# Position tables over 194 distinct columns, and table pieces of five and three tiles, in a DeBERTa-style attention kernel

## The chip, the cores and the metric

The kernel runs on one core of a Trainium2 chip. The metric is the device time of one execution in microseconds (us). The kernel before was timed three times: 1996.8 us in the median, from 1993.77 to 2002.08 us.

## What is computed

A sandwich layer over x of shape (4, 1024, 256) in fp32: attention with relative positions inside two layer norms, then a mixture of eight experts chosen by argmax inside two more. What matters here is the attention's position term, for 16 heads of 16 channels:

```python
scores = einsum('bhqd,bhkd->bhqk', q, k) / scale
rel = log_bucket(q_index - k_index)            # exact up to 32, logarithmic up to 127, then flat
c2p = take_along_axis(q @ pos_k.T, clip(rel + 64, 0, 127))
p2c = take_along_axis(k @ pos_k.T, clip(-rel + 64, 0, 127)).swapaxes(-1, -2)
probs = softmax(scores + (c2p + p2c) / scale)
ctx = einsum('bhqk,bhkd->bhqd', probs, v)
```

`rel` depends on the distance alone. Between distances -31 and 31 the reference puts every distance into one and the same bucket, so the position term is flat there; beyond 127 it is a constant on each side.

## The kernel before

The program is five blocks that run one after the other: `spread` (position rows), `project` (q, k, v), `attend`, `mix` (output projection, norms, routing) and `experts`. The change lies in `spread` and `attend`.

**The unit of work in attend.** A unit n is one (batch, head) pair; there are 64, each of eight tiles of 128 queries (or keys). Scores have a band: for query tile t the key tiles t-1, t, t+1 need the position term by distance, and all others take the constant of their side through extra rows of the bf16 products. A step s of the main loop stands for tile t = s % 8 of unit n = s // 8.

**Tables.** For a tile of 128 queries (and one of 128 keys) PE multiplies with the picked position rows and gets, for 255 distances and one far column, two tables of 128 x 256 in PSUM (`make_table`, L703 to L715). This runs 16 steps ahead of the scores (AHEAD). ScalarE (ACT) copies both tables to SBUF (`keep_table`, L852 to L859), between the two halves of the exponent of another tile.

**The skew.** A table holds distances; a score tile needs them by key, shifted by one column a row. The shift is made through DRAM: SyncE (SP) writes tables to `skew_d` (`skew_write`) and reads them back with a row pitch one element shorter (`skew_read`) into `near`. A unit has two pieces: the writes cover tiles 0 to 3 and 4 to 7 (1024 KB each), the reads tiles 0 to 2 and 3 to 7 (384 KB and 640 KB for each of two tables). In what follows W0, W1 are the two writes of a unit and R0, R1 the two reads (each of two DMAs). SP's order in a round u (L677 to L695) is R1 of unit u+1, W0 of u+2, the loads of unit u+4, the store of u-2, R0 of u+2, W1 of u+2. SP handles one DMA after the other and stands at each wait: a read waits until its write has landed in DRAM (`skew_out`, L662), a write until its last tile's table is copied (`table_kept`, L651).

**Edges.** GpSimd (POOL) makes the triangular edges of `near` in five operations for each piece (`edge`, steps 0 to 4), the first behind the read's landing (`skew_in`, L925); the tuple `steps` (L964) says at which step s of the round each is put in POOL's order. At t = 7 POOL also splits the row maxima of the unit into three bf16 parts (`split_top`), behind whatever edge operations stand before it.

**Scores and probabilities.** PE makes the scores of step s (`score`), adds `near` for keys by transposing products (L740, which waits for the piece's edges by `near_made`), VectorE (DVE) finds the maxima and adds `near` for queries (`look`, `level`), and 13 steps later PE turns the result (`flip`), ACT takes the exponent in two halves of 512 (`exponent`), and PE multiplies with v (`weigh`, one step later). The maxima come back as three rows of the products: at t = 1 PE turns the split maxima of the unit before (`turn_top`, L782, which waits for `split_made` and shares `table_ps` with the tables) and ACT copies them (`keep_top`).

PE's order in a step is flip half 0, a table, flip half 1, scores, weigh, and at t = 1 `turn_top`. Each engine runs its own list in order and stands at each wait.

Of the kernel before, what the change touches and what calls it, by code (L numbers as in the profile page):

```python
# [30 lines left out]
BAND = 2 * P - 1  # L31
PARTS = 3
# [21 lines left out]
def constants():  # L54
# [14 lines left out]
    pick[:, right, BAND] -= 1  # L69
    k, m = np.arange(P)[:, None], np.arange(P)[None, :]  # L70
# [19 lines left out]
def build(nc, x, Wq, bq, Wk, bk, Wv, bv, Wo, bo, rel_emb, ln_s, ln_b, W1, b1, W2, b2, Wr, br,  # L90
          c_pick, c_masks, c_fold, c_side, c_steps, c_sel, out):
    ctx = ExitStack()
    with ctx:
# [10 lines left out]
        pick_d = dram("pick_d", [KROWS, H * 4 * P], BF16)  # L104
# [64 lines left out]
def spread(nc, sem, Wk, bk, rel_emb, c_pick, c_masks, c_side, pick_d, posT_d):  # L169

    with ExitStack() as ctx:
# [8 lines left out]
        pick = sb("pick", [P, 2, 2 * P])  # L180
# [17 lines left out]
        def _(sp):  # L198
# [9 lines left out]
            for tab in range(2):  # L208
                for n, (first, step, many) in enumerate((KSLOTS, QSLOTS)[tab]):
                    for slot in range(first, first + step * many, step):  # L210
                        for c in range(2):
                            sp.dma_start(view(pick_d, slot * (DH * H * 4 * P) + c * 8 * 4 * P + tab * 2 * P,
                                              [[4 * P, 8], [H * 4 * P, DH], [1, 2 * P]]),
                                         part[:, n, tab, c, :]).then_inc(stored, 16)
# [4 lines left out]
        def _(pe):  # L219
# [10 lines left out]
            for c in range(2):  # L230
                nc.tensor.transpose(posT_ps[:, c, :], pos[:, c * P:(c + 1) * P], ident)
                for tab in range(2):
                    last = nc.tensor.matmul(pick_ps[:, tab, c, :], pos[:, c * P:(c + 1) * P], pick[:, tab, :],
# [4 lines left out]
        def _(act):  # L238
# [7 lines left out]
            for tab in range(2):  # L246
                last = nc.scalar.copy(pick32[:, tab, :, :], pick_ps[:, tab, :, :])
# [307 lines left out]
def attend(nc, sem, spent, c_masks, split_d, far_d, v_d, pick_d, skew_d, ctx_d):  # L555
# [12 lines left out]
    PIECES = ((0, 3), (3, QT))  # L568
    EDGES = ((0, 3), (3, QT - 1))
# [4 lines left out]
    with ExitStack() as ctx:  # L574
# [10 lines left out]
        rows = sb("rows", [KROWS, H, 2, 2 * P], BF16)  # L585
        vals = [sb(f"vals{i}", [P, QT, VROW]) for i in range(2)]
        table = [sb(f"table{i}", [P, 2, 2, 4, SPOT]) for i in range(2)]
# [41 lines left out]
        def _(sp):  # L629
# [20 lines left out]
            def skew_write(n, h):  # L650
                sp.wait_ge(table_kept, n * QT + 4 * h + 4)  # L651
                if n >= 2:
                    sp.wait_ge(skew_in[n % 2][0], 16 * 2 * (n // 2))
                    sp.wait_ge(skew_in[n % 2][1], 16 * 2 * (n // 2))
                sp.dma_start(view(skew_d, n % 2 * (P * PITCH) + h * 4 * SPOT + 1, [[PITCH, P], [TABLE, 2], [1, 4 * SPOT]]),
                             table[n % 2][:, h, :, :, :].rearrange("p a u v -> p a (u v)")).then_inc(skew_out[n % 2][h], 16)

            def skew_read(n, h):
                if n >= 2:
                    sp.wait_ge(scored, (n - 2) * QT + 4 * h + 4)  # L660
                    sp.wait_ge(seen, (n - 2) * QT + 4 * h + 4)
# [38 lines left out]
        def _(pe):  # L700
            ident = masks[:, 4, :]

            def make_table(x):  # L703
# [8 lines left out]
                nc.tensor.matmul(table_ps[:, 0, :], quest[i][0:KROWS, u * P:(u + 1) * P], rows[:, n % H, 0, :],  # L712
                                 start=True, stop=False)
                nc.tensor.matmul(table_ps[:, 1, :], after[i][0:KROWS, u * P:(u + 1) * P], rows[:, n % H, 1, :],  # L714
# [925 lines left out]
```

## Time and profile before

| | us |
|---|---|
| median of three runs | 1996.8 |
| lowest, highest | 1993.77, 2002.08 |
| the profiled execution | 2003.63 |
| its span, first to last instruction | 2001.7 |
| PE busy | 1698.0 (85%) |
| DVE busy | 1370.7 (68%) |
| ACT busy | 1121.8 (56%) |
| POOL busy | 1069.1 (53%) |
| q1, SP's DMA queue, share of 16 DMA engines | 65.2% |

The profiled execution is one of its own, 1.9 us longer than its span. "Busy" of PE counts matmuls in flight, which overlap. The tables begin at 215 us and the last weighted sum of attend is copied at about 1490 us, so attend takes 1275 us of the 2002.

### The profile page before, as it was taken

The numbers are of one execution on the slowest core, as the hardware profiler recorded it, in microseconds if no ns is written. First come the engines' busy times: TensorE is split into PE (matmuls) and PEld (weight loads), VectorE is DVE, ScalarE is ACT, GpSimd is POOL, SyncE is SP. The second block draws the span as 40 slices with busy tenths as digits, with TensorE's granted clock in tenths as the row PEclk, the third lists the DMA queues.
The fourth block names the chain that finished last, engine by engine and source line by source line (L and its number), as shares of the span: only waits on it lengthen the run. The fifth ranks groups of instructions, "written<-read, shape, count | busy, mean of one in ns | idle before, by whom it ended". The sixth has DMA issues, their size and how long they took to land. (4 is left out here: it accounts for less than half of the span.)

```text
span 2001.7 us, 40568 instructions
## 1 busy us (share of the span) xinstructions
PE 1698.0 (85%) x13688; PEld 1159.6 (58%) x13688; DVE 1370.7 (68%) x3938; ACT 1121.8 (56%) x2233; POOL 1069.1 (53%) x1268
## 2 busy tenths in 40 slices
PE   1882389999999999999999999999973674999997
PEld 1451156565656566566565666566532464999996
DVE  1673188788888788898798899899843553343343
ACT  1672257676767677677677777677751460222221
POOL 0210267676777667667576777777711451233332
PEclk6996589999999999999999999999996675999998
DMA  4598778777777777777877777787718852676772
GB/s 113 188 303 274 225 250 262 246 237 251 245 261 248 256 247 240 257 254 245 265 237 251 249 261 250 240 272 246 235 44 215 284 176 86 198 212 215 223 219 78
DMA packets 320826, 453.36 MB, mean 226 GB/s; under 512 B 35132, under 2 KB 260303, under 8 KB 320526
## 3 DMA queue, kind: packets, MB, share of 16 engines
q1 hardware_dynamic: 308034, 415.25, 65.2%
q10 hardware_dynamic: 7596, 21.10, 3.4%
q0 software_dynamic: 4992, 14.43, 1.9%
q8 instruction: 112, 1.84, 0.4%
q14 instruction: 92, 0.75, 0.1%
HBM read 257.32 MB, written 193.65 MB: 225 GB/s over the span
## 5 line engine op out<-in xcount | busy, mean ns | idle before, releaser
L865 ACT ACTIVATE t_probsT<-t_flip 128x512 f32<-128x512 f32 x1024 | 619.2, 607 | 242.7 <-PE t_flip L756 117.5
L814 DVE TENSOR_REDUCE t_most<-t_scores 128x1 f32<-128x640 f32 (+1 forms) x512 | 436.7, 853 | 169.8 <-PE t_scores L740 166.5
L833 DVE TENSOR_SCALAR t_band<-t_band,t_top 128x384 f32<-128x384 f32 (+1 forms) x512 | 383.8, 750 | 0.0
L859 ACT COPY t_table<-t_table_ps 128x512 f32<-128x512 f32 x512 | 298.2, 582 | 70.7 <-issue 41.1
L777 PE MATMUL t_sum_ps<-t_probsT,t_vals 128*32 128x256 f32 x4096 | 329.5, 394 | 0.2 <-ACT t_probsT L865 0.2
L926 POOL TENSOR_TENSOR t_near<-t_near,t_masks 128x384 f32<-128x384 f32 (+1 forms) x128 | 146.8, 1147 | 338.9 <-DMA t_near<-skew_d 336.4
L942 POOL TENSOR_TENSOR t_near<-t_near,t_masks 128x768 f32<-128x768 f32 (+1 forms) x128 | 272.4, 2129 | 0.0
L763 PE MATMUL t_flip<-t_masks,t_band 128*128 128x128 f32 x1408 | 263.0, 276 | 0.0
L818 DVE CUSTOM_DVE_ANT_0 t_band<-t_scores,t_near 128x384 f32<-128x384 f32 (+1 forms) x512 | 262.1, 512 | 0.0
L740 PE MATMUL t_scores<-t_masks,t_near 128*128 128x128 f32 x1408 | 243.5, 277 | 7.1 <-POOLq L945 7.1
L733 PE MATMUL t_scores<-t_after,t_quest 105*128 105x256 bf16 (+3 forms) x1024 | 244.9, 289 | 2.6 <-DVE t_most L818 2.4
L740 PEld LDWEIGHTS t_scores<-t_masks,t_near 128*128 128x128 f32 x1408 | 182.7, 143 | 46.6 <-POOLq L945 8.7
L712 PE MATMUL t_table_ps<-t_rows,t_quest 96*128 96x256 bf16 x512 | 143.5, 280 | 69.1 <-DMA t_before<-far_d 49.8
L733 PE MATMUL t_scores<-t_before,t_quest 105*128 105x256 bf16 (+3 forms) x768 | 195.0, 294 | 0.0
L763 PEld LDWEIGHTS t_flip<-t_masks,t_band 128*128 128x128 f32 x1408 | 164.7, 143 | 4.8
L756 PE MATMUL t_flip<-t_quest,t_before 108*128 108x512 bf16 (+3 forms) x512 | 161.4, 316 | 0.8 <-ACT t_probsT L865 0.7
L756 PE MATMUL t_flip<-t_quest,t_after 108*128 108x512 bf16 (+3 forms) x512 | 158.7, 310 | 1.2 <-DMA t_quest<-t_topT 0.8
L1606 PE MATMUL e_hid_ps<-e_xT,e_w 128*128 128x128 f32 x1248 | 148.0, 278 | 5.6 <-DMA e_total<-total_d 5.2
L1606 PEld LDWEIGHTS e_hid_ps<-e_xT,e_w 128*128 128x128 f32 x1248 | 147.5, 194 | 8.2 <-issue 5.5
L939 POOL TENSOR_TENSOR t_near<-t_near,t_masks 128x384 f32<-128x384 f32 (+1 forms) x128 | 145.5, 1137 | 0.0
L714 PE MATMUL t_table_ps<-t_rows,t_after 96*128 96x256 bf16 x512 | 142.9, 279 | 0.0
L1588 PE MATMUL e_out_ps<-w_all,e_hid 128*128 x624 | 141.0, 379 | 0.0
(186 smaller groups left out, 2343.7 us busy)
## 6 DMA issues: line engine op xcount, KB each, us to landing
skew_d<-t_table SPq DMA_DIRECT2D x128, 1024.0 KB, 8.9
t_near<-skew_d SPq DMA_DIRECT2D x128, 640.0 KB, 6.2
t_near<-skew_d SPq DMA_DIRECT2D x128, 384.0 KB, 4.8
e_w<-in_L_ffn_W_dram ACTq DMA_DIRECT2D x39, 512.0 KB
e_w<-in_L_ffn_W_dram SPq DMA_DIRECT2D x39, 512.0 KB
split_d<-p_part SPq DMA_DIRECT2D x32, 384.0 KB
t_after<-split_d SPq DMA_DIRECT2D x64, 192.0 KB
t_quest<-split_d SPq DMA_DIRECT2D x64, 192.0 KB
```

The source lines that it names most:

```text
L733: nc.tensor.matmul(out[:, at:at + size], quest[i][0:XROWS, t * P:(t + 1) * P], keys[0:XROWS, piece[0] * P:piece[0] * P + size], start=at % ...
L740: last = nc.tensor.matmul(out[:, (j - lo) * P:(j - lo + 1) * P], near[n % 2][:, 1, j, (t - j + 1) * P:(t - j + 2) * P], ident, start=False ...
L756: last = nc.tensor.matmul(out[:, (a - lo) * P:(z - lo) * P], keys[:, j * P:(j + 1) * P], quest[i][:, a * P:z * P], start=first, stop=False ...
L763: last = nc.tensor.matmul(out[:, (t - lo) * P:(t - lo + 1) * P], band[n % 2][:, t, at:at + P], ident, start=False, stop=True, is_transpose ...
L777: last = nc.tensor.matmul(sum_ps[32 * g:32 * g + 32, 0:2 * P], vals[b % 2][:, j, h * VDIM:h * VDIM + 32], probsT[s % 3][:, g * 2 * P:(g + ...
L814: nc.vector.tensor_reduce(most[:, c, 1:2], out[:, wide:S], AX.X, ALU.max)
L818: nc.vector.tensor_tensor_reduce(band[n % 2][:, t, 0:wide], out[:, 0:wide], near[n % 2][:, 0, t, at:at + wide], 1.0, -3.0e38, ALU.add, ALU ...
L833: nc.vector.tensor_scalar(band[n % 2][:, t, 0:wide], band[n % 2][:, t, 0:wide], top[n % 2][:, t:t + 1], None, ALU.subtract).then_inc(level ...
L859: nc.scalar.copy(table[n % 2][:, h, :, u % 4, :], table_ps[:, :, :]).then_inc(table_kept, 1)
L865: nc.scalar.activation(probsT[s % 3][:, half * 512:(half + 1) * 512], flip_ps[half][:, :], ACT.Exp, scale=SCALE).then_inc(expd, 1)
L942: nc.gpsimd.tensor_tensor(tail, tail, masks[:, 1, :].unsqueeze(1).unsqueeze(1).to_broadcast([P, 2, many, P]), ALU.mult).then_inc(edge_made, 1)
L1606: last = nc.tensor.matmul(hid_ps[s % 2][:, c, :], w1[s % WB][:, f, c * P:(c + 1) * P], xT[s % 2][:, f, :], start=(f == 0), stop=(f == 1))
```

## The change

It has five parts.

1. `spread` and `make_table` work with 194 columns of each table in place of 256: 97 from each end. Columns 96 to 158 (63 of them) are all alike, since the buckets are flat there.
2. `keep_table` writes the same 256 columns to SBUF as before, by two ACT copies in place of one: the two ends (2 x 2 x 97 = 388 elements a partition), and the 62 middle columns of both tables out of one PSUM column each, by a broadcast read (124 elements).
3. The writes cover tiles 0 to 4 and 5 to 7, the reads tiles 0 to 3 and 4 to 7, and the edges go with the reads (four tiles' edges, then three).
4. POOL's order: `keep_side` of the first piece at t = 5, the first piece's edges at steps 3 to 6 and the second's at 7, 8 and 9. Before `split_top` at t = 7 stand two edge operations of the second piece, where three stood.
5. The waits of PE and DVE for the second piece of `near` come at t = 4, where they came at t = 3. All else in attend, with `mix` and `experts`, stays.

```diff
+FLAT = SPAN // 2 - 1
+LEFT = P - FLAT
+FEW = 2 * LEFT
...
+    assert (pick[:, :, LEFT - 1:2 * P - LEFT] == pick[:, :, LEFT - 1:LEFT]).all()
+    pick = np.concatenate([pick[:, :, :LEFT], pick[:, :, 2 * P - LEFT:]], 2)
...
-        pick32 = sb("pick32", [P, 2, 2, 2 * P])
-        rest = sb("rest", [P, 2, 2, 2 * P])
-        part = sb("part", [P, PARTS, 2, 2, 2 * P], BF16)
+        pick32 = sb("pick32", [P, 2, 2, FEW])
+        rest = sb("rest", [P, 2, 2, FEW])
+        part = sb("part", [P, PARTS, 2, 2, FEW], BF16)
...
-    PIECES = ((0, 3), (3, QT))
-    EDGES = ((0, 3), (3, QT - 1))
+    TILES = ((0, 5), (5, QT))
+    PIECES = ((0, 4), (4, QT))
+    EDGES = ((0, 4), (4, QT - 1))
...
-                sp.wait_ge(table_kept, n * QT + 4 * h + 4)
+                lo, hi = TILES[h]
+                sp.wait_ge(table_kept, n * QT + hi)
...
-                nc.tensor.matmul(table_ps[:, 0, :], quest[i][0:KROWS, u * P:(u + 1) * P], rows[:, n % H, 0, :],
+                nc.tensor.matmul(table_ps[:, 0, 0:FEW], quest[i][0:KROWS, u * P:(u + 1) * P], rows[:, n % H, 0, :],
...
-                pe.wait_ge(near_made, n * 2 + (1 if t < 3 else 2))
+                pe.wait_ge(near_made, n * 2 + (1 if t < 4 else 2))
...
-                nc.scalar.copy(table[n % 2][:, h, :, u % 4, :], table_ps[:, :, :]).then_inc(table_kept, 1)
+                wide = table[n % 2][:, :, u, :]
+                ends = view(wide.tensor, wide.offset, [list(wide.ap[0]), list(wide.ap[1]), [SPOT - LEFT, 2], [1, LEFT]])
+                nc.scalar.copy(ends, table_ps[:, :, 0:FEW].rearrange("p a (e v) -> p a e v", e=2))
+                nc.scalar.copy(wide[:, :, LEFT:SPOT - LEFT],
+                               table_ps[:, :, LEFT - 1:LEFT].to_broadcast([P, 2, SPOT - FEW])).then_inc(table_kept, 1)
...
-            steps = ((2, 0, (0, 1)), (3, 0, (2,)), (4, 0, (3,)), (5, 0, (4,)),
-                     (6, 1, (0, 1)), (7, 1, (2,)), (8, 1, (3,)), (9, 1, (4,)))
+            steps = ((3, 0, (0, 1)), (4, 0, (2,)), (5, 0, (3,)), (6, 0, (4,)), (7, 1, (0, 1)), (8, 1, (2, 3)), (9, 1, (4,)))
...
-                if t == 4 and 0 <= u + 2 < N:
+                if t == 5 and 0 <= u + 2 < N:
                     keep_side(u + 2, 0)
```

## Rows read from the trace of the kernel before

**Rows 1.** Busy time by stretch: stretch, its length, engines (count), PE clock, DMA share, GB/s.

```profile
1200.00:1400.00 200.00, 193.49 (x1789) 122.32 (x1791) 179.93 (x511) 149.10 (x287) 143.82 (x177) 0.99 0.76 252
```

**Rows 2.** Waits of SP's queue, whole span: us in total, times, longest us.

```profile
SPq L662 <- DMA skew_d<-t_table: 726.6, 120, 8.3
...
SPq L655 <- ACT t_table L859: 11.3, 11, 6.9
```

**Rows 3.** Timeline of SP's issues, one round in mid-run: start, us, engine, line, operation.

```profile
1010.50 1.19 SPq L665 DMA_DIRECT2D t_near<-skew_d  x2
1011.79 0.56 SPq L655 DMA_DIRECT2D skew_d<-t_table  x1
...
1021.33 0.91 SPq L665 DMA_DIRECT2D t_near<-skew_d  x2
1022.35 0.57 SPq L655 DMA_DIRECT2D skew_d<-t_table  x1
1029.70 0.93 SPq L665 DMA_DIRECT2D t_near<-skew_d  x2
1030.74 0.56 SPq L655 DMA_DIRECT2D skew_d<-t_table  x1
```

**Rows 4.** The same timeline, W0 of unit 1, and the last rounds without loads.

```profile
235.76 0.56 SPq L655 DMA_DIRECT2D skew_d<-t_table  x1
...
1410.50 1.39 SPq L665 DMA_DIRECT2D t_near<-skew_d  x2
...
1420.37 0.89 SPq L665 DMA_DIRECT2D t_near<-skew_d  x2
...
1428.42 0.93 SPq L665 DMA_DIRECT2D t_near<-skew_d  x2
```

**Rows 5.** Waits of the engines, whole span: us in total, times, longest us.

```profile
POOL t_near L926 <- DMA t_near<-skew_d: 336.4, 114, 6.1
...
PEld t_table_ps L785 <- POOL t_top_part L962: 78.1, 54, 5.2
```

**Rows 6.** POOL's timeline: first edge operation of R1's piece, then first and last split.

```profile
999.76 1.28 POOL L926 TENSOR_TENSOR t_near<-t_near,t_masks 128x512 f32<-128x512 f32 x1 [6.10 <-DMA t_near<-skew_d]
...
1003.10 0.25 POOL L952 CAST t_top_part<-t_top 128x8 bf16<-128x8 f32 x1
...
1004.23 0.19 POOL L962 CAST t_top_part<-t_top_rest 128x8 bf16<-128x8 f32 x1
```

**Rows 7.** PE's timeline: position products of the first tile of two units.

```profile
1019.58 0.38 PE L740 MATMUL t_scores<-t_masks,t_near 128*128 128x128 f32 x2
...
1037.74 0.38 PE L740 MATMUL t_scores<-t_masks,t_near 128*128 128x128 f32 x2
```

**Rows 8.** Groups by line and shape: busy us, mean ns of one, idle before.

```profile
L859 ACT COPY t_table<-t_table_ps 128x512 f32<-128x512 f32 x512 | 298.2, 582 | 70.7 <-issue 41.1 <-PE t_table_ps L714 29.7
...
L733 PE MATMUL t_scores<-t_after,t_quest 105*128 105x256 bf16 x576 | 145.5, 276 | 0.9 <-DVE t_most L818 0.7
...
L733 PE MATMUL t_scores<-t_after,t_quest 105*128 105x128 bf16 x192 | 42.7, 223 | 1.7 <-DVE t_most L818 1.7
...
L885 ACT COPY t_made<-t_sum_ps 128x256 f32<-128x256 f32 x64 | 23.8, 372 | 12.2 <-PE t_sum_ps L777 12.2
```

**Rows 9.** DMA issues in 300 to 1380 us: count, KB each, median us to landing.

```profile
t_near<-skew_d SPq DMA_DIRECT2D x112, 384.0 KB, 4.8
```

**Rows 10.** ACT's timeline, two table copies while attend fills.

```profile
220.46 0.58 ACT L859 COPY t_table<-t_table_ps 128x512 f32<-128x512 f32 x1 [0.70 <-PE t_table_ps L714]
...
221.75 0.58 ACT L859 COPY t_table<-t_table_ps 128x512 f32<-128x512 f32 x1 [0.70 <-PE t_table_ps L714]
```

**Rows 11.** Timeline of spread: a pair of pick products, a cast, the stores.

```profile
13.60 1.57 PE L233 MATMUL s_pick_ps<-s_pick,s_pos 128*128 128x256 f32 x4
...
16.38 1.04 ACT L250 CAST s_part<-s_pick 128x1024 bf16<-128x1024 f32 x1
...
21.04 14.85 SPq L212 DMA_DIRECT2D pick_d<-s_part  x24
```

More of the change, by code:

```diff
@@ L179, in spread @@
         bk_row = sb("bk_row", [1, D])
-        pick = sb("pick", [P, 2, 2 * P])
+        pick = sb("pick", [P, 2, FEW])
         masks = sb("masks", [P, 5, P])
@@ L232, in _ @@
                 for tab in range(2):
-                    last = nc.tensor.matmul(pick_ps[:, tab, c, :], pos[:, c * P:(c + 1) * P], pick[:, tab, :],
+                    last = nc.tensor.matmul(pick_ps[:, tab, c, 0:FEW], pos[:, c * P:(c + 1) * P], pick[:, tab, :],
                                             start=True, stop=True)
@@ L246, in _ @@
             for tab in range(2):
-                last = nc.scalar.copy(pick32[:, tab, :, :], pick_ps[:, tab, :, :])
+                last = nc.scalar.copy(pick32[:, tab, :, :], pick_ps[:, tab, :, 0:FEW])
             last.then_inc(act_made, 1)
@@ L584, in attend @@
         quest, after, before = ([sb(f"{w}{i}", [ROWS, S], BF16) for i in range(BUFS)] for w in ("quest", "after", "before"))
-        rows = sb("rows", [KROWS, H, 2, 2 * P], BF16)
+        rows = sb("rows", [KROWS, H, 2, FEW], BF16)
         vals = [sb(f"vals{i}", [P, QT, VROW]) for i in range(2)]
-        table = [sb(f"table{i}", [P, 2, 2, 4, SPOT]) for i in range(2)]
+        table = [sb(f"table{i}", [P, 2, QT, SPOT]) for i in range(2)]
         side = [sb(f"side{i}", [P, 2, QT]) for i in range(2)]
@@ L654, in skew_write @@
                     sp.wait_ge(skew_in[n % 2][1], 16 * 2 * (n // 2))
-                sp.dma_start(view(skew_d, n % 2 * (P * PITCH) + h * 4 * SPOT + 1, [[PITCH, P], [TABLE, 2], [1, 4 * SPOT]]),
-                             table[n % 2][:, h, :, :, :].rearrange("p a u v -> p a (u v)")).then_inc(skew_out[n % 2][h], 16)
+                sp.dma_start(view(skew_d, n % 2 * (P * PITCH) + lo * SPOT + 1, [[PITCH, P], [TABLE, 2], [1, (hi - lo) * SPOT]]),
+                             table[n % 2][:, :, lo:hi, :].rearrange("p a u v -> p a (u v)")).then_inc(skew_out[n % 2][h], 16)
             def skew_read(n, h):
                 if n >= 2:
-                    sp.wait_ge(scored, (n - 2) * QT + 4 * h + 4)
-                    sp.wait_ge(seen, (n - 2) * QT + 4 * h + 4)
+                    sp.wait_ge(scored, (n - 2) * QT + TILES[h][1])
+                    sp.wait_ge(seen, (n - 2) * QT + TILES[h][1])
                 sp.wait_ge(skew_out[n % 2][h], 16 * (n // 2 + 1))
@@ L711, in make_table @@
                     pe.wait_ge(top_kept, (x - AHEAD) // QT)
-                nc.tensor.matmul(table_ps[:, 0, :], quest[i][0:KROWS, u * P:(u + 1) * P], rows[:, n % H, 0, :],
+                nc.tensor.matmul(table_ps[:, 0, 0:FEW], quest[i][0:KROWS, u * P:(u + 1) * P], rows[:, n % H, 0, :],
                                  start=True, stop=False)
-                nc.tensor.matmul(table_ps[:, 1, :], after[i][0:KROWS, u * P:(u + 1) * P], rows[:, n % H, 1, :],
+                nc.tensor.matmul(table_ps[:, 1, 0:FEW], after[i][0:KROWS, u * P:(u + 1) * P], rows[:, n % H, 1, :],
                                  start=False, stop=True).then_inc(table_made, 1)
@@ L910, in keep_side @@
             def keep_side(n, h):
[L911 removed]
+                lo, hi = TILES[h]
+                pool.wait_ge(table_kept, n * QT + hi)
                 if n >= 2:
[L913 to L914 removed]
+                    pool.wait_ge(edge_made, (n - 2) * 10 + 10)
+                nc.gpsimd.tensor_copy(side[n % 2][:, :, lo:hi], table[n % 2][:, :, lo:hi, BAND]).then_inc(side_kept, 1)
             def edge(n, h, step):
```

15 lines of the change are left out of this document (6 added, 9 removed).

## The prediction

> **What bounds the kernel now.** I read the busy time by stretch first. In mid-attend PE is busy 193.5 us of 200, DVE 179.9, ACT 149.1, and the DMA engines 76% [rows 1]. That looks like a kernel bound by PE, and the change takes PE columns away. But busy PE is not PE at its peak, so I went on to the waits.
>
> The second view is the waits of SP's own queue. SP stood 726.6 us for the landing of its writes to `skew_d`, 120 times, and only 11.3 us for a table that was not yet copied [rows 2]. A queue that hardly ever waits for compute isn't fed late by compute: it sets its own pace. The third view, SP's timeline, shows that pace [rows 3]. W0 is issued at 1011.79; R0 at 1021.33, 9.54 us later, when W0 has landed; W1 1.02 us after that, at 1022.35; R1 at 1029.70, 7.35 us later, when W1 has landed; the next W0 at 1030.74. The loop closes in 18.95 us, and no edge of it is compute: it is two write landings and two issues of a pair of reads. From W0 of unit 1 at 235.76 [rows 4] to W0 of unit 41 at 1011.79 [rows 3] it took 776.03 / 40 = 19.40 us a unit, and from R1 at 1010.50 [rows 3] to R1 at 1428.42, 22 units on [rows 4], 19.00. The mean over these 62 is 19.26 us.
>
> The fourth view is who waits behind that loop. POOL waits 336.4 us for the reads [rows 5]; its three edge operations run from 999.76 to 1003.10, the split of the maxima ends at 1004.42 [rows 6]; and PE's `turn_top` waits 78.1 us for that split in 54 of the units [rows 5]. Where PE does not wait, a unit takes it 18.16 us, from 1019.58 to 1037.74 [rows 7]. So PE could do a unit in 18.16 us and gets its data every 19.26 us. The DMA loop is the bound; PE's wait at `turn_top` is where the difference is spent.
>
> **Columns of the table products.** 128 fewer bf16 columns shorten a matmul's time from 276 to 223 ns [rows 8], so 62 fewer shorten it by 53 x 62/128 = 26 ns, two a tile 0.05 us, a unit 0.41 us. PE's own unit goes from 18.16 to 17.75 us. This lies wholly under the DMA loop: worth 0 in the steady part. It would be 64 x 0.41 = 26 us if PE set the pace.
>
> **Two ACT copies for one.** 512 columns take 582 ns and 256 take 372 [rows 8]: 0.82 ns a column and 162 ns fixed. 388 columns are 480 ns, 124 are 264. Between no more than before (if the second hides its fixed part) and +0.16 us, I take +0.08 us a tile, the middle, since nothing in the trace puts two copies back to back. ACT is busy 149 of 200 us [rows 1]; 83 tiles fall in such a stretch (200 / 19.26 x 8), so it goes to 156 or at most 162 of 200. The cover is ACT's 25% of idle time. If that were gone it would be 512 x 0.16 = 83 us. What is queued behind the second copy is the exponent's other half, for which PE's next `flip` waits; that is compute ahead of a DMA loop with 1.1 us a unit to spare.
>
> The Trainium skill (ScalarE: Activation LUTs, What ACT_TABLE_LOAD costs) gives an instruction with immediate scale and bias 186 ns plus 0.833 ns an element, and lets neighbours overlap by about 93 ns. The trace agrees on the slope (0.82) and has 162 for the 186. By the page a further copy would take 93 ns of ACT, 48 us over 512 tiles, none of it on the path by the argument above.
>
> **Pieces of five and three tiles.** This is what touches the bound. Bytes in a unit stay: 2 x 1024 KB written, 2 x 1024 KB read. They move between the loop's halves. Half A is R1, then W0 behind it: 1010.50 to 1021.33 = 10.83 us. Half B is R0, then W1: 1021.33 to 1029.70 = 8.37 us [rows 3]. They differ by 512 KB of reads, and by the loads behind W0. In the last rounds, without loads, half A is 1410.50 to 1420.37 = 9.87 and half B 1420.37 to 1428.42 = 8.05 [rows 4]: 512 KB of reads cost 1.82 us, so 256 KB cost 0.91. A write: the second DMA of R0 is issued about 0.46 us after 1021.33 and lands after 4.8 [rows 9], at 1026.6; W1 has landed at 1029.6; 1024 KB in 3.0 us, 256 KB in 0.75. New half A: -0.91 + 0.75 = -0.16. New half B: +0.91 - 0.75 = +0.16. Sum 0.00 us a unit, because everything here is linear in bytes. The bound on that: with loads the halves differ by 2.46, not 1.82, so 0.64 us a unit is not told by bytes. If it came from the long read and both halves now paid it, the loop would grow by 0.64, 62 x 0.64 = 40 us; if neither paid it, the loop would lose the same. I take 0: loads stay behind W0, and with them the surcharge. Half of the bound, 20 us, goes into the range.
>
> W0 now waits for a fifth table, one step later. For unit 42 that table is made in the fifth step of unit 40, whose first tile stands at 1019.58 [rows 7]: four steps of 18.16 / 8 = 2.27 us, 0.4 for `turn_top` (an estimate) and 0.5 for the copy put it at 1029.6, and SP reaches W0 at 1030.74 [rows 3]. The margin is 1.1 us, and PE moves forward against the loop by what `turn_top` gains, next. Worth 0; without that margin each us of lateness would lengthen the loop by as much, 62 us in all.
>
> **The earlier split.** Three operations over four tiles take 3.34 us before the split [rows 6]. Two over three tiles are about 3.34 x 2/3 x 3/4 = 1.7 us, and R1 of four tiles lands 0.9 us sooner, so the split ends 2.5 us earlier against the loop. PE waits 78.1 / 54 = 1.4 us there, so that wait goes. What is late next is the same data: PE runs ahead by those 2.5 us once, and then stands for `near` or for the split of the next unit, at the pace of the loop. A wait that is moved forward in phase is paid back once, at the end: after the last R1, PE's tail of unit 63 and the 13 steps behind it begin 2.5 us earlier. -2.5 us. POOL's first piece now has four tiles, but its result is needed a whole piece later; 0.
>
> **Filling.** Tables follow each other by 221.75 - 220.46 = 1.29 us [rows 10]. W0 of unit 0 needs five: +1.3 us, and carries 256 KB more with no shortened read ahead of it: +0.75, and half B +0.16. +2.2 us.
>
> **Spread.** Two pairs of pick products of 1.57 us [rows 11] lose 62/256: -0.8. Five passes over 1024 columns (L247 as two halves, L250, L252, L263, L265), 1.04 us each by the cast, lose a quarter: 5 x 0.25 = -1.3. The 24 stores take 14.85 us to issue, 0.62 each [rows 11], whatever they carry: 0. Together -2.1 us.
>
> The Trainium skill (DMA: Bandwidth & Descriptors, Specifications) asks for at least 512 B a transfer, below which the DMA engine reads, modifies and writes. Store runs fall from 512 to 388 B here. It speaks against the change, yet only for these 24 stores in the shadow of their issue; no row of this kernel shows what it costs.
>
> **Sum.** -2.5 + 2.2 - 2.1 = -2.4 us on the profiled 2003.6 (span 2001.7), so 2001.2 for an execution like it. Against the median, which is 6.8 us below the profiled one, 1996.8 - 2.4 = 1994.4 us.
>
> **Rivals.** *PE is the bound after all.* For it: 193.5 of 200 us busy. Then each unit falls from 19.26 to 17.75, 62 x 1.51 = 94 us, and the time is 1900. Against it: SP's rows, in which no issue waits for a table. 6%. *The loop shortens:* the evened reads lose part of the 0.64 us; half of it is 20 us, 1974. For it: the halves with long reads are the dear ones. 22%. *The loop lengthens:* reads of four tiles in both halves each pay the surcharge; half of it is +20 us, 2014, from the point at which the surcharge belongs to any read of over three tiles. 16%. It is the one that ends slower. *The split does not come sooner,* since POOL stands for R1 before it in both versions: then the tail's 2.5 us are missing, 1997. 5%. The forecast itself has 51%.
>
> **How the numbers follow.** A measurement of this kernel can tell about 0.5%, 10 us. The forecast and the unmoved split fall inside it: 0.56. Shorter loop and PE bound: 0.28. Longer loop: 0.16. The range leaves out the PE rival and the outer parts of the two loop cases: 1977 to 2011.
>
> **What would show it.** If right: SP's loop still closes in 18.9 to 19.3 us with waits of L655 for tables near zero; half A about 10.7 and half B about 8.5; the wait at L785 is gone and PE waits in its place elsewhere, behind DMA or POOL, some 1.5 us a unit; PE's busy time falls by 20 us or more with the span unchanged. Wrong: W latencies whose sum changes by over 0.2 us a unit, or SP waiting for tables for tens of us, which would mean that compute was the pacer.

## The result and the profile after

The changed kernel takes 2031.5 us in the median of four runs (2027.3 to 2037.8), the kernel before 1998.8 with a run of it beside these. The ratio is 1.017, 95% interval 1.013 to 1.021. It is slower by 33 us; forecast were 1994.4 us and a range up to 2011. The profiled execution takes 2030.25 us with a span of 2028.3, against 2003.63 and 2001.7.

The first view is SP's timeline: W0 of unit 1, one round in mid-run, and R1 of unit 62 (start, us, engine, line, operation). It answers to [rows 3, 4].

```profile
233.97 0.56 SPq L662 DMA_DIRECT2D skew_d<-t_table  x1
...
1014.78 0.57 SPq L662 DMA_DIRECT2D skew_d<-t_table  x1
1023.75 0.91 SPq L672 DMA_DIRECT2D t_near<-skew_d  x2
1024.77 0.56 SPq L662 DMA_DIRECT2D skew_d<-t_table  x1
1034.87 0.93 SPq L672 DMA_DIRECT2D t_near<-skew_d  x2
1035.91 0.57 SPq L662 DMA_DIRECT2D skew_d<-t_table  x1
...
1458.29 0.91 SPq L672 DMA_DIRECT2D t_near<-skew_d  x2
```

From W0 of unit 1 to R1 of unit 62 the loop takes 1458.29 - 233.97 = 1224.32 us, or / 62 = 19.75 us a unit. The same two issues before stand at 235.76 and 1428.42 [rows 4]: 19.24. I use this measure, "the loop", for every kernel below. It is 0.51 us a unit longer, 62 x 0.51 = 32 us. The span grew by 26.6: the loop also begins 1.8 us earlier, the tail is 1.8 us shorter, and the rest is in the blocks that the change doesn't touch. So the whole loss lies in the DMA loop, and the stages around it brought a little.

Next the waits of SP's queue and of the other engines (us in total, times, longest us), beside [rows 2, 5]:

```profile
SPq L669 <- DMA skew_d<-t_table: 679.4, 117, 8.5
SPq L662 <- ACT t_table L869: 24.0, 33, 9.9
...
POOL t_near L938 <- DMA t_near<-skew_d: 367.0, 128, 8.6
...
PEld t_table_ps L792 <- POOL t_top_part L974: 105.2, 61, 3.3
```

SP still waits for landings (679 us) and hardly for tables (24 us, of which the fill's 9.9 is one). No compute moved into the loop. But PE's wait for the split at `turn_top` (L792) did not go: 105 us, where it was 78. Then the DMAs by size in 300 to 1380 us (count, KB each, median us to landing), of after first and of before below, the same view as [rows 9]:

```profile
t_near<-skew_d SPq DMA_DIRECT2D x220, 512.0 KB, 5.9
skew_d<-t_table SPq DMA_DIRECT2D x55, 1280.0 KB, 9.0
skew_d<-t_table SPq DMA_DIRECT2D x55, 768.0 KB, 7.9
```

```profile
skew_d<-t_table SPq DMA_DIRECT2D x112, 1024.0 KB, 9.2
t_near<-skew_d SPq DMA_DIRECT2D x112, 640.0 KB, 6.4
```

A read of 512 KB takes 5.9 us; the middle of the old 4.8 and 6.4 is 5.6. Both reads of a unit now take nearly as long as the long one did. The short write gained nothing: 768 KB behind a read of 512 KB lands after 7.9 us, where W1 of before, 1024 KB behind a read of 384 KB, had landed within 7.35 us of its issue [rows 3].

### The profile page after: what moved, and what is told of

The parts are those of the page before. It is cut to its first block and busy times, and to the rows that moved or that the text cites. A ratio compares the mean times of both kernels' runs of the same rounds, so it can differ in the third digit from the quotient of the medians.

```text
span 2028.3 us, 41080 instructions
## 1 busy us (share of the span) xinstructions
PE 1692.7 (83%) x13688; PEld 1151.7 (57%) x13688; DVE 1401.9 (69%) x3938; ACT 1151.0 (57%) x2745; POOL 1071.6 (53%) x1268
## 5 line engine op out<-in xcount | busy, mean ns | idle before, releaser
L840 DVE TENSOR_SCALAR t_band<-t_band,t_top 128x384 f32<-128x384 f32 (+1 forms) x512 | 423.9, 828 | 0.0
L938 POOL TENSOR_TENSOR t_near<-t_near,t_masks 128x512 f32<-128x512 f32 (+1 forms) x128 | 147.2, 1150 | 367.0 <-DMA t_near<-skew_d 367.0
L868 ACT COPY t_table<-t_table_ps 128x388 f32<-128x388 f32 x512 | 247.3, 483 | 71.1 <-issue 40.9
L954 POOL TENSOR_TENSOR t_near<-t_near,t_masks 128x1024 f32<-128x1024 f32 (+1 forms) x128 | 271.9, 2124 | 0.0
L719 PE MATMUL t_table_ps<-t_rows,t_quest 96*128 96x194 bf16 x512 | 130.6, 255 | 68.5 <-DMA t_before<-far_d 46.5
L951 POOL TENSOR_TENSOR t_near<-t_near,t_masks 128x512 f32<-128x512 f32 (+1 forms) x128 | 146.9, 1147 | 0.0
L869 ACT COPY t_table<-t_table_ps 128x124 f32<-128x124 f32 x512 | 143.4, 280 | 0.0
```

Source lines behind the costliest of these rows:

```text
L840: nc.vector.tensor_scalar(band[n % 2][:, t, 0:wide], band[n % 2][:, t, 0:wide], top[n % 2][:, t:t + 1], None, ALU.subtract).then_inc(level ...
L954: nc.gpsimd.tensor_tensor(tail, tail, masks[:, 1, :].unsqueeze(1).unsqueeze(1).to_broadcast([P, 2, many, P]), ALU.mult).then_inc(edge_made, 1)
```

## The experiments

Each kernel is compared with the kernel before, in runs on the same chip: that is its ratio, with its 95% interval. The loop comes from one profiled execution each. The executions of one kernel spread over 3 to 22 us, which is 0.05 to 0.35 us a unit, and the kernel before itself took 1999 to 2016 us in the median beside the different groups of runs. Where two kernels of different groups stand less than about 0.3 us a unit apart, their ratios decide and not their loops.

### One part at a time

**e1** has the columns, the two copies and the spread of the change, with the old pieces, waits and order. It also keeps the change's layout of `table` in SBUF (`[P, 2, QT, SPOT]`, all eight tiles of one table in a row). The diff is against the changed kernel.

```diff
-    TILES = ((0, 5), (5, QT))
-    PIECES = ((0, 4), (4, QT))
-    EDGES = ((0, 4), (4, QT - 1))
+    TILES = ((0, 4), (4, QT))
+    PIECES = ((0, 3), (3, QT))
+    EDGES = ((0, 3), (3, QT - 1))
```

> The 194 columns and the two ACT copies, with the pieces (writes 4+4 tiles, reads 3+5) and POOL's order of before. Theory S (the even reads of 4+4 tiles slow the loop) and theory P (compute that runs 2.5 us earlier against the loop slows the reads): no change, 1994 to 2000 us, SP's loop at 19.2 us a unit, PE's wait at the turn of the maxima as before or 0.4 us longer. Theory C (the second ACT copy or the short products slow something): about 2030.

1964.5 us, ratio 0.980 (0.977 to 0.982), beside 2004.5 for the kernel before. Loop 18.63 us a unit:

```profile
233.97 0.56 SPq L662 DMA_DIRECT2D skew_d<-t_table  x1
...
1389.20 0.93 SPq L672 DMA_DIRECT2D t_near<-skew_d  x2
```

The part that I had priced at nothing brings 40 us, and it brings them in the DMA loop, to which it adds no wait and from which it takes none. This kernel beats both the kernel before and the changed one.

**e2** has the pieces and the order alone, with 256 columns and one copy.

```diff
+    TILES = ((0, 5), (5, QT))
+    PIECES = ((0, 4), (4, QT))
+    EDGES = ((0, 4), (4, QT - 1))
```

> Writes 5+3, reads 4+4 and POOL's new order, with 256 columns and one ACT copy. Theories S and P: the whole loss, 2027 to 2034 us, loop 19.7 us a unit. Theory C: 1997.

2073.9 us, ratio 1.035 (1.029 to 1.040); loop 20.26. The pieces and the order alone cost 1.02 us a unit. The change is a gain and a larger loss added up.

**e3** is the kernel before with the second piece's edges in the new order.

```diff
-                     (6, 1, (0, 1)), (7, 1, (2,)), (8, 1, (3,)), (9, 1, (4,)))
+                     (7, 1, (0, 1)), (8, 1, (2, 3)), (9, 1, (4,)))
```

> The kernel before with POOL's order alone changed: two edge operations of the second piece ahead of the split in place of three. Transfers untouched. The split ends about 1 us earlier against the loop. Theory P: part of the loss, 2005 to 2020 us, with the reads' landing later. Theory S: no change or 1 us less, 1995 to 2000, loop 19.2.

2006.7 us, ratio 1.001 (1.000 to 1.003); loop 19.26. The order by itself is worth nothing with the old pieces.

**e4** is the changed kernel with the reads, and the edges and waits that go with them, back at three and five tiles; the writes stay at five and three.

```diff
-    PIECES = ((0, 4), (4, QT))
-    EDGES = ((0, 4), (4, QT - 1))
+    PIECES = ((0, 3), (3, QT))
+    EDGES = ((0, 3), (3, QT - 1))
```

> The changed kernel with reads (and edges, and the waits for them) of 3+5 tiles as before, writes still 5+3. Theory S: the loop returns to 19.2 us or less, 1992 to 2002 us. Theory P: the split is still early, so the loss stays, 2020 to 2035 us. If the writes of 5 and 3 tiles are the cause, also 2025 or more.

1974.8 us, ratio 0.985 (0.982 to 0.988); loop 18.88. From here to the changed kernel is one step, the evened reads, and it costs 0.87 us a unit. From e1 to here are the writes of five and three with the order, 0.25; by the ratios that is 0.5% and at the edge of what the runs can tell. The evened reads are 3.2% by the ratios and far beyond it. The DMAs by size of e1, then of e4:

```profile
skew_d<-t_table SPq DMA_DIRECT2D x116, 1024.0 KB, 8.8
t_near<-skew_d SPq DMA_DIRECT2D x116, 640.0 KB, 6.1
t_near<-skew_d SPq DMA_DIRECT2D x115, 384.0 KB, 4.6
```

```profile
t_near<-skew_d SPq DMA_DIRECT2D x114, 640.0 KB, 6.0
skew_d<-t_table SPq DMA_DIRECT2D x57, 1280.0 KB, 9.7
t_near<-skew_d SPq DMA_DIRECT2D x116, 384.0 KB, 4.5
skew_d<-t_table SPq DMA_DIRECT2D x57, 768.0 KB, 6.3
```

In e4 the write behind the short read (768 KB) lands after 6.3 us, in the changed kernel after 7.9: the landing of a write moves with the size of the read ahead of it. And e1's transfers have the sizes of before, yet each is 0.2 to 0.4 us faster than before's 9.2, 6.4 and 4.8. Something other than their size made them faster.

### What makes e1 faster

Three things could: shorter products, copies that are placed otherwise, or where `skew_d` lies in DRAM. `pick_d` is allocated ahead of it, and with 194 columns it is 96 x 16 x 124 x 2 B = 372 KB smaller, so `skew_d` moves down by as much. **f2** is e1 with `pick_d` given its old size, of which the rest is unused.

```diff
-        pick_d = dram("pick_d", [KROWS, H * 2 * FEW], BF16)
+        pick_d = dram("pick_d", [KROWS, H * 4 * P], BF16)
```

> The kernel of columns alone with pick_d given its old size in DRAM, so that skew_d behind it keeps the address it had before. Theory A (the gain of the columns is the skew buffer's new place in DRAM): the gain goes, 1997 to 2004 us, loop 19.2. Otherwise 1964, loop 18.6.

2010.9 us, ratio 1.005 (1.003 to 1.007); loop 19.36.

```profile
234.22 0.56 SPq L662 DMA_DIRECT2D skew_d<-t_table  x1
...
1434.37 0.93 SPq L672 DMA_DIRECT2D t_near<-skew_d  x2
```

No engine's work in attend differs from e1 (the one load of the position rows skips the unused part), and the gain is gone, with a little more. So the new layout of `table`, which f2 has as well, brings nothing either. **f3** is the kernel before with two ACT copies for one, **f4** with products of 194 columns; f4 leaves the tables' columns from 194 on unmade, so it doesn't compute the position term.

```diff
-                nc.scalar.copy(table[n % 2][:, h, :, u % 4, :], table_ps[:, :, :]).then_inc(table_kept, 1)
+                nc.scalar.copy(table[n % 2][:, h, :, u % 4, 0:194], table_ps[:, :, 0:194])
+                nc.scalar.copy(table[n % 2][:, h, :, u % 4, 194:SPOT], table_ps[:, :, 194:SPOT]).then_inc(table_kept, 1)
```

```diff
+                few = 2 * P if x == 0 else 194
+                nc.tensor.matmul(table_ps[:, 0, 0:few], quest[i][0:KROWS, u * P:(u + 1) * P], rows[:, n % H, 0, 0:few],
```

> The kernel before with each table copied by two ACT copies (2x194 and 2x62 columns), products of 256 columns. If the gain of the columns comes from how ACT writes the tables: about 1970, loop 18.7. If it costs what a second instruction costs and lies under the loop: 1997 to 2004.

> The kernel before with table products of 194 columns (from the second tile on; columns 194 to 255 of the tables keep what the first product left, so the position terms are not those of the reference). One ACT copy of 512 as before. If PE's shorter unit is what sped the loop: about 1965 to 1975, loop 18.6. If PE lies under the loop as forecast: 1997 to 2004, loop 19.2.

Ratios 1.002 (1.001 to 1.004) and 1.003 (1.001 to 1.004), loops 19.29 both. Neither part of the compute is worth anything, as forecast; 0.2 to 0.3% are lost to each. The 40 us come from what lies behind `pick_d` in DRAM. f2 moves `skew_d` together with two small buffers behind it; the next runs move `skew_d` alone.

### The transfers alone

**g1** and **g3** put a stage ahead of attend in which SP runs the loop (writes, reads and two loads a unit, waits for landings only) and no other engine works; the rest of the program follows as in e1. Old place means `skew_d` shifted back by those 372 KB.

```diff
+            for tiles, pieces, pitch, off in configs:
...
+                for u in range(-2, UNITS):
+                    if 0 <= u + 1 < UNITS:
+                        read(u + 1, 1)
+                    if 0 <= u + 2 < UNITS:
+                        write(u + 2, 0)
+                        load(u + 2)
+                        read(u + 2, 0)
+                        write(u + 2, 1)
```

> The kernel of columns alone with a stage put in ahead of attend in which SP runs its loop (read 1, write 0, two loads of 192 KB, read 0, write 1) with no compute beside it, eight units in each of nine settings. Settings, in order: old DRAM place of the skew buffer (372 KB higher) with reads 3+5 tiles and writes 4+4; the same place, reads 4+4 and writes 5+3; the new place with the same two; the new place with reads 3+5 and writes 5+3; 3+5 and 4+4 at 8 KB above the new place; the same at 128 KB above it; a row pitch of 4160 elements in place of 4096 with the first two kinds. Theory S (even reads are slow in themselves): about 0.5 to 1 us a unit between kinds at one place, here too. Theory P (they are slow only beside compute that runs early): no difference between the kinds here, and 0.5 us or more a unit under the 18.6 to 19.7 of attend. Theory A (the place in DRAM): 0.6 us between the old and the new place here too; if it shows only beside compute, it is no matter of the skew buffer's own rows.

In g1, W1 of a unit also waited for R0 of that unit, which attend doesn't ask for, and it had only eight units a setting. Its periods: 20.07 us at the old place with reads of three and five tiles, 20.73 with the changed pieces; 19.01 and 19.89 at the new place, and 19.27 there with writes of five and three and reads of three and five. With the old pieces a shift of the buffer by 8 KB from the new place made it 18.99 and by 128 KB 19.54; rows 4160 elements apart for 4096 made it 18.40 with the old pieces and 18.59 with the changed ones. g3 has the wait as attend has it, and 16 units a setting.

> As the first kernel with SP's loop alone, but write 1 no longer waits for read 0 of its own unit, as in attend, and sixteen units in each of eight settings: old place with reads 3+5 and writes 4+4; old place, reads 4+4 and writes 5+3; new place with the same two; new place, reads 3+5 and writes 5+3; row pitch 4160 with the first two kinds; row pitch 4352 with the first. If the transfers alone carry the differences of attend: old against new place 0.4 to 0.6 us a unit, even reads against 3+5 at writes 5+3 0.6 to 0.9. What attend's 18.6 (columns alone) and 19.7 (changed kernel) stand above the settings three and four is what compute costs the loop: theory P expects more for the fourth.

SP's timeline of g3, the issue of W0 of unit 1 and of unit 15 of four settings: old place, old pieces; old place, changed pieces; new place, old pieces; new place, changed pieces.

```profile
220.55 0.54 SPq L199 DMA_DIRECT2D skew_d<-b_table  x1
...
480.27 0.55 SPq L199 DMA_DIRECT2D skew_d<-b_table  x1
...
520.63 0.55 SPq L199 DMA_DIRECT2D skew_d<-b_table  x1
...
795.69 0.55 SPq L199 DMA_DIRECT2D skew_d<-b_table  x1
...
834.50 0.55 SPq L199 DMA_DIRECT2D skew_d<-b_table  x1
...
1082.91 0.55 SPq L199 DMA_DIRECT2D skew_d<-b_table  x1
...
1122.45 0.55 SPq L199 DMA_DIRECT2D skew_d<-b_table  x1
...
1383.45 0.55 SPq L199 DMA_DIRECT2D skew_d<-b_table  x1
```

Divided by 14 units: 18.55, 19.65, 17.74 and 18.64 us. Within a setting the periods differ by 0.5 to 1.3 us from the shortest to the longest, and the means of its first and second half by at most 0.2. With no compute at all the place is worth 0.81 to 1.01 us a unit and the pieces cost 0.90 to 1.10. Writes of five and three with reads of three and five, at the new place, took 17.91: of the pieces' 0.90, 0.17 are the writes and 0.73 the evened reads. Last, the distance of the rows of `skew_d`: 4160 elements apart for 4096, the changed pieces take 17.93 for 18.64, the old ones 18.15 for 17.74, and 4352 apart the old ones take 18.32. The sign for the old pieces is the other way round than in g1 (18.40 for 19.01), so it hangs on something in which the two differ, the waits between the transfers or the chip.

**g4** asks whether an engine at work in SBUF slows the transfers: the changed pieces alone, then beside POOL, DVE, ACT and PE, each busy throughout with operations on tiles of its own.

```diff
+                nc.gpsimd.tensor_tensor(own["g"][1][:, 0:1024], own["g"][0][:, 0:1024], own["g"][0][:, 0:1024], ALU.mult).then_inc(step["g"], 1)
```

> SP's loop as in the run before at the new place, twelve units in each of six settings: reads 4+4 and writes 5+3 with no compute, then with POOL, DVE, ACT and PE busy, one at a time, on tiles of their own; last, reads 3+5 with none. If an engine's SBUF traffic slows transfers, its setting is 0.3 us a unit or more above the first; if contention needs the same tiles or DRAM, all are within 0.2.

18.62 alone, 18.45 beside POOL, 18.45 beside DVE, 18.46 beside ACT, 19.13 beside PE; the old pieces alone, at the end, 17.74. W0 of unit 1 and of unit 11, alone and then beside PE:

```profile
224.77 0.54 SPq L247 DMA_DIRECT2D skew_d<-b_table  x1
...
410.96 0.55 SPq L247 DMA_DIRECT2D skew_d<-b_table  x1
...
1262.63 0.55 SPq L247 DMA_DIRECT2D skew_d<-b_table  x1
...
1453.89 0.55 SPq L247 DMA_DIRECT2D skew_d<-b_table  x1
```

POOL, DVE and ACT do not slow the loop. PE does, by 0.5 us a unit, more than the 0.3 that I had set as the mark: five of its ten periods are 19.35 to 19.91 us, and of the forty periods of the other four settings with these pieces none is above 18.94. PE is busy 83% of the changed kernel, so this is a part of what attend stands above the transfers alone. Why PE's work does it, and whether two engines at once do more, no run separates.

### What is left over: the phase

Alone, the whole change is worth 18.64 - 18.55 = +0.09 us a unit; in attend it is +0.51. So 0.42 arise only with the compute beside the transfers. One thing that the change does to the compute is to bring it forward against them: the phase. **f1** and **g2** are the changed kernel with the split later again: behind all five operations of the second piece, and behind four.

```diff
-            steps = ((3, 0, (0, 1)), (4, 0, (2,)), (5, 0, (3,)), (6, 0, (4,)), (7, 1, (0, 1)), (8, 1, (2, 3)), (9, 1, (4,)))
+            steps = ((3, 0, (0, 1)), (4, 0, (2,)), (5, 0, (3,)), (6, 0, (4,)), (7, 1, (0, 1, 2, 3, 4)))
```

```diff
+            steps = ((3, 0, (0, 1)), (4, 0, (2,)), (5, 0, (3,)), (6, 0, (4,)), (7, 1, (0, 1, 2, 3)), (8, 1, (4,)))
```

> The changed kernel with all five edge operations of the second piece ahead of the split, so that PE turns the maxima some 3.5 us later against SP's loop than in the changed kernel. Theory S (reads of 4+4 tiles are slow in themselves): loop still 19.7 us a unit, 2031 us. Theory P (compute that runs early against the loop slows the reads): loop back towards 18.9, 1975 to 2000 us.

1990.7 us, ratio 0.993 (0.991 to 0.996); loop 18.89. The latest split gives the fastest version with these pieces and this row distance. Its waits of SP:

```profile
SPq L662 <- ACT t_table L869: 62.3, 62, 10.4
```

Now W0 waits for its fifth table in nearly every round, and comes a median 1.75 us behind R1 for 1.01. W0 lands after 7.92 us for 9.05, and half A takes 9.84 for 10.40 in the mean of units 8 to 57. I had priced such lateness at its full length, 62 us for each us; here the loop with a wait for compute in it is the shorter one. That the wait itself shortens it is not shown, since all compute stands later too.

> The changed kernel with four edge operations of the second piece ahead of the split (two in the changed kernel, all five in the run before), so that PE stands about 2 us later against SP's loop, and SP still never waits for a table. Theory P: loop 19.0 to 19.3 us, about 1990 to 2000 us. Theory S with a gain in the late-split run that came from W0 being issued later: loop 19.7, 2025 to 2035.

2006.1 us, ratio 1.001 (0.999 to 1.003); loop 19.30, W0 without a wait (1.01 behind R1). Against the changed kernel that is 0.45 us a unit, or 1.6% by the ratios, from two operations of POOL that stand ahead of the split. Transfers, sizes and place are the same. VectorE's load is not what does it: g2 has more of it (busy 1418.5 us for 1401.9) and is the faster one.

ScalarE's small DMA of the turned maxima was a suspect. In the changed kernel it leaves within about 1 us of R0's issue, before or behind it, in the median 0.4 us behind; in g2 2.3 behind and in f1 4.5. **k1** sends it one step later, **k2** moves `turn_top` with the copy and the DMA one step later.

```diff
-                if s > QT and s % QT == 1 and s // QT <= N:
-                    turn_top(s // QT - 1)
+                if s > QT and s % QT == 2 and s // QT <= N:
+                    turn_top(s // QT - 1)
```

> The changed kernel with one difference: the DMA that ScalarE issues for the turned maxima (L890) goes out one step (2.3 us) later, behind the next tile's table copies, so that it no longer falls within 0.6 us of the issue of read 0 but about 2.5 us behind it, where it falls in the kernel before and in the late split. PE, POOL and the split keep their early phase. Theory A (the early phase costs time because this small DMA enters the queue's engines together with the pair of read 0): the loop falls from 19.75 to about 19.3 us a unit and the time from 2031 to about 2006. Theory B (the early phase costs through what the engines do in SBUF, or through the place of the transfers against compute as a whole): loop 19.7 to 19.8, time 2028 to 2034.

> The changed kernel with PE's turn of the maxima (turn_top), ScalarE's copy of them and its DMA one step later (t = 2 in place of 1), while POOL's split stays where it is. PE then no longer stands at turn_top, or stands less: it runs up to 2.3 us earlier against SP's loop until it stands for the near of a piece. Theory A (the DMA of the maxima beside read 0 is the cost): that DMA leaves at nearly the same place against the loop as in the changed kernel, or a little later; time 2010 to 2031. Theory B (the earlier compute stands against the loop, the slower the transfers): loop 19.8 to 20.2 us, time 2035 to 2060. If PE's waiting at turn_top were the price itself, the time would fall to 2006 or less.

k1: 2037.2 us, ratio 1.011 (1.007 to 1.015), loop 19.73. k2: 2022.4 us, ratio 1.003 (1.001 to 1.005), loop 19.56. The kernel before took 2016.2 us beside both, 17 us more than the 1998.8 of the changed kernel's ratio, so the ratios must be read here and not the loops. By them k2 wins back nearly all of the 1.6% and stands beside g2; k1 wins back a third, with an interval that overlaps the changed kernel's. R0 and the small DMA in one round of k1, k2 and g2 (ScalarE's and SP's timelines):

```profile
1035.16 0.93 SPq L672 DMA_DIRECT2D t_near<-skew_d  x2
1035.83 0.73 ACTq L892 DMA_DIRECT2D t_quest<-t_topT  x1
...
1036.13 0.93 SPq L672 DMA_DIRECT2D t_near<-skew_d  x2
1039.45 0.73 ACTq L890 DMA_DIRECT2D t_quest<-t_topT  x1
...
1020.23 0.93 SPq L672 DMA_DIRECT2D t_near<-skew_d  x2
1022.51 0.73 ACTq L890 DMA_DIRECT2D t_quest<-t_topT  x1
```

k1 did not bring the DMA where it was meant to go: in the median it leaves 1.2 us behind R0, where the expectation had 2.5. The five kernels with the same transfers, in medians over the units:

| kernel | ratio | small DMA behind R0's issue, us | W0 behind its fifth table, us |
|---|---|---|---|
| changed | 1.017 | 0.4 | 4.0 |
| k1 | 1.011 | 1.2 | 4.4 |
| k2 | 1.003 | 2.7 | 3.6 |
| g2 | 1.001 | 2.3 | 1.6 |
| f1 | 0.993 | 4.5 | 0.0 |

"The earlier the compute, the slower" does not hold as it stands: in k2 POOL's split and the tables are nearly as early as in the changed kernel, and its time is that of g2. The time goes with the place of the maxima's turn and of its small DMA. That is a correlation over five kernels: the DMA, ScalarE's copy and PE's turn and wait move together in it, and no run moves the DMA alone by 2 us. That the phase costs 0.45 us a unit is shown by g2; by what it does so is open, with the small DMA beside R0 not excluded.

### The row pitch

g1 had suggested 4160 elements between rows, by 0.61 us a unit with the old pieces and 1.30 with the changed ones. **h1** is e1, **h2** the changed kernel, with that pitch.

```diff
-    PITCH = 2 * TABLE
+    PITCH = 2 * TABLE + 64
```

> The kernel of columns alone with a row pitch of 4160 elements in the skew buffer (the gaps are filled once in spread). Theory A (it is how the rows lie in DRAM that sets the pace): the loop falls by the 0.6 us of the transfers alone, to 18.0 us, and the time to about 1930 us; PE's own unit of 17.75 us is the floor. If attend does not follow the transfers alone: 1964.

> The changed kernel with a row pitch of 4160 elements. By the transfers alone the loop falls by 1.0 to 1.3 us, to 18.5 us, and the time from 2031 to about 1955 us; the even reads then cost less than 0.3 us a unit against the columns alone with this pitch.

h1: 1975.7 us, ratio 0.982 (0.980 to 0.985), loop 18.84. h2: 1998.5, ratio 0.993 (0.991 to 0.995), loop 19.13 for 19.75. The kernel before took 2012.3 us beside both. Against the changed kernel h2 gains 2.4% by the ratios, 0.77 us a unit and 0.62 by the loops, as g3 has it with the transfers alone (-0.71). h1 can't be told from e1 (0.980, 0.977 to 0.982), so the +0.41 that g3 has for it is not shown in attend; the gain of 0.61 that g1 had for it did not come. My expectations of 1930 and 1955 had promised more because they rest on g1, which has a wait that attend doesn't have. The lowest time is e1's, 1964.5 us.

## Why the prediction was wrong, step by step

**The bound: right.** SP's loop of two landings and two reads sets the pace; only f1 has a wait for compute in nearly every round of it. Where the loop moved, the time moved, and the parts of the compute (f3, f4) were worth 0 to +0.3%.

**Columns and copies as compute: right.** The table products fell as worked out, and the second copy costs less than I took. ACT's and PE's groups by line of after (busy, mean ns | idle before), beside [rows 8]:

```profile
L868 ACT COPY t_table<-t_table_ps 128x388 f32<-128x388 f32 x512 | 247.3, 483 | 71.1 <-issue 40.9 <-PE t_table_ps L721 30.2
L869 ACT COPY t_table<-t_table_ps 128x124 f32<-128x124 f32 x512 | 143.4, 280 | 0.0
L721 PE MATMUL t_table_ps<-t_rows,t_after 96*128 96x194 bf16 x512 | 131.3, 256 | 0.0
```

A product went from 279 to 256 ns (26 forecast, 23 measured), the copies are 483 and 280 ns (480 and 264 forecast). ACT's timeline of after shows the pair:

```profile
1281.30 0.48 ACT L868 COPY t_table<-t_table_ps 128x388 f32<-128x388 f32 x1
1281.66 0.28 ACT L869 COPY t_table<-t_table_ps 128x124 f32<-128x124 f32 x1
1281.82 0.63 ACT L876 ACTIVATE t_probsT<-t_flip 128x512 f32<-128x512 f32 x1
```

From the start of the first copy to that of the exponent behind the second are 0.36 + 0.16 = 0.52 us, against 0.46 to 0.47 for one copy before: about +0.05 us a tile where I took +0.08. They overlap by 0.12 us. The Trainium skill (ScalarE: Activation LUTs, What ACT_TABLE_LOAD costs) has about 93 ns of overlap; this pair shows more. I also forecast that PE's busy time would fall by 20 us or more; it fell by 5.3, to 1692.7 (83%). The products gave 24.5 us; most groups of flips, sums and scores took 2 to 3 ns longer a matmul, and busy counts them while in flight. That sign was badly chosen.

**"Worth 0" for the smaller tables: the first step that failed.** I listed what `spread` loads and stores, and never asked what the allocation behind `pick_d` becomes. The place of `skew_d` is worth -0.61 us a unit in attend (before to e1) and -0.81 alone. The trace of before could not show it. It hid about half of the loss: without it the change costs e2's 1.035 in place of 1.017. e2 keeps the old place of `skew_d`.

**Pieces, "sum 0.00, because everything here is linear in bytes": the second, and the one that set the sign.** I had seen 0.64 us a unit that bytes don't tell, asked whether it belonged to the long read, and gave 16% to "reads of four tiles in both halves each pay the surcharge". That is what happened, by more than the surcharge: +0.73 alone (17.91 to 18.64), +0.87 in attend (e4 to after). The term that was mis-sized is the read. From e4 to after, R1 gives 256 KB to R0 and nothing else moves; in the mean of units 8 to 57 half A goes from 11.12 to 10.42, -0.70 where I had -0.91, and half B from 7.75 to 9.32, +1.57 where I had +0.91. So shortening the long read gave less than its bytes, and lengthening the short one cost 1.7 times its bytes. The writes came nearer: from e1 to e4, with the order, half A grows by 0.80 and half B shrinks by 0.54, for 0.75 each.

I had also read the 0.64 us wrongly. It rested on one of the two rounds without loads; the other has half A at 10.36 us, and the means leave 0.2 us (halves apart by 2.32 us in units 8 to 57, by 2.09 in the two rounds without loads). And I had put it on the loads, "and with them the surcharge". The cost of evened reads does not hang on the loads: in the same two last rounds, without them, the loop takes 19.05 us in the changed kernel and 18.37 in e4. Writes of five and three add 0.17 alone, with the order 0.25 in attend; I had 0 for that as well. Why two pairs of reads of 512 KB cost more than one of 384 and one of 640 is not settled: the pitch changes it (18.64 to 17.93 with even reads, 17.74 to 18.15 with uneven ones), so the pattern of addresses has a part in it, and no run says more.

**The fifth table: no wait, as forecast.** W0 comes 4.1 us after its fifth table is kept, where I had 1.1; SP waits 24 us for tables in all. In f1, where W0 did come late, the loop was shorter and not longer by the lateness; the price that I gave to it, its full length, did not hold there.

**The earlier split: half right.** It ends 3.25 us behind R1's landing in the mean, for 4.73. POOL's timeline of after, beside [rows 6]:

```profile
1009.22 1.01 POOL L938 TENSOR_TENSOR t_near<-t_near,t_masks 128x384 f32<-128x384 f32 x1 [1.50 <-DMA t_near<-skew_d]
...
1011.07 0.19 POOL L964 CAST t_top_part<-t_top 128x8 bf16<-128x8 f32 x1
1012.23 0.19 POOL L974 CAST t_top_part<-t_top_rest 128x8 bf16<-128x8 f32 x1
```

1.85 us from the first edge operation to the first split, for 3.34, as the sum had it (1.7). The tail from R1 of unit 62 to the last score fell from 41.8 to 40.0 us: -1.8 for -2.5. What failed is "so that wait goes": PE moves forward and then stands at the same place, since the split remains the last thing that a unit needs from R1. And its 0 for the steady part was wrong, the third step: with two operations of POOL ahead of the split in place of four the transfers are slower by 0.45 us a unit (g2), which is 28 of the 33 us that were lost. No rival had that. Which part of the earlier work does it is open.

**Filling and spread: the sum right, by offset.** Forecast were +2.2 and -2.1 us. W0 of unit 1 is issued 1.8 us earlier, but that issue scatters by 1 to 2 us from one kernel to the next where filling and spread are the same. In the mean it comes at 235.4 us in the four kernels with neither part (before, e3, f3, f4), at 233.8 with the spread alone (e1, f2, h1) and at 235.2 with both (the changed kernel, e4, f1, g2, h2, k1, k2): -1.7 for the spread, +1.4 for the filling. Spread's part shows in the issue of the stores, beside [rows 11]:

```profile
19.30 14.85 SPq L217 DMA_DIRECT2D pick_d<-s_part  x24
```

It begins 1.74 us earlier and takes the same 14.85 us with runs of 388 B for 512, and the next block's first load follows 1.64 us behind the last store's issue, for 1.72 before. The Trainium skill (DMA: Bandwidth & Descriptors, Specifications) speaks against runs under 512 B; neither the issue nor the wait behind it shows any of it.

**The range.** The uncertain term had a bound of 40 us on either side, and I put half of it in the range without giving a ground; my own rival of 2014 us lay above the range's end of 2011. With the whole bound the range would have reached to about 2034 and held the time. That would have been partly luck, since the time is a sum of +0.87, +0.25 and -0.61 us a unit, of which the last had no term at all, and +0.87 is more than the bound of 0.64.

## What to carry to other kernels

Where a loop of strided DMAs sets the pace, its price is not its bytes: re-cutting the same bytes cost 0.9 us of 18, so such a cut wants a run of the transfers by themselves, which here gave each single step (place, writes, evened reads, pitch) to within 0.3 us a unit, though not the phase against the compute. Such a run must have the kernel's own waits: g1, with one wait more, promised gains from the pitch that the kernel did not give. A change that resizes any DRAM buffer moves the ones behind it; hold their addresses when two versions are compared, and try the address as a setting of its own. Bringing forward compute that only waits for such a loop gains nothing in the steady part, and here went with slower transfers. Compare versions by their ratio to a kernel run beside them: the same kernel took 1999 to 2016 us in different groups.

## What the runs showed of the hardware that I had not expected

- The place of a DRAM buffer: the same writes and reads take 18.55 us a unit at one address and 17.74 us 372 KB lower, with all compute engines idle (g3), and 19.36 and 18.63 in attend (f2 against e1, ratios 1.005 and 0.980).
- The distance of its rows: 4160 for 4096 elements takes 0.71 us from a unit with even reads (g3; 0.77 in attend by the ratios of h2). With reads of three and five tiles it adds 0.41 in g3 and takes 0.61 in g1, which has one wait more between the transfers and ran on another chip.
- POOL, DVE or ACT, busy alone beside the transfers, do not slow them (18.45 to 18.46 for 18.62, g4); PE does (19.13). In attend the loop takes 0.25 to 1.2 us a unit more than the same transfers alone.
- A write issued 0.7 us later behind a pair of reads landed 1.1 us sooner (f1: 7.92 for 9.05 us in the median), in a kernel whose compute stands later as well.
